# Channel maxima in one reduction per step: a gated mixture-of-experts kernel over NCHW images

## The reference

```python
def _L0_conv_ref(x, conv_w, conv_b):
    pooled = jnp.stack([jnp.max(x, axis=1), jnp.mean(x, axis=1)], axis=1)
    y = conv3x3(pooled, conv_w) + conv_b
    return x * jax.nn.sigmoid(y)

x = x + _L0_conv_ref(_ln_c(x), ...)
t = _to_tokens(x)
t = t + _L0_ffn_ref(_ln_t(t), ...)
```

## Time and profile before

| | us |
|---|---|
| median of 3 runs | 1582.37 (1581.99 to 1584.48) |
| the profiled execution, its own time | 1582.87 |
| its span, first to last instruction | 1581.1 |
| TensorE busy | 1432.2 |
| VectorE busy | 1326.6 |
| ScalarE busy | 1084.0 |
| GpSimd busy | 1072.8 |
| VectorE waiting for TensorE's spreads (line 665 for line 468) | 154.0 |
| TensorE waiting for VectorE's units (line 468 for line 665) | 91.0 |

### The profile page before, as it was taken

The page is one execution under the profiler, slowest core; times in us unless marked ns, Lnnn a source line. Parts: engine busy times, 40 slices in busy tenths (PEclk is TensorE's granted clock), DMA queues, the critical chain, the costliest instruction groups (busy, mean ns, idle before and its releaser), DMA issues.

```text
span 1581.1 us, 34381 instructions
## 1 busy us (share of the span) xinstructions
PE 1432.2 (91%) x12198; PEld 673.0 (43%) x12198; DVE 1326.6 (84%) x1647; ACT 1084.0 (69%) x4061; POOL 1072.8 (68%) x729
## 2 busy tenths in 40 slices
PE   8855998999898999899988998989998888899998
PEld 8753444444444444444434443444443232233333
DVE  6776898888898888889888888988888888887676
ACT  6667887778777887778877787778887334344432
POOL 5234776767676676677667676766766668787675
PEclk9955999999999999999999999999999899999999
DMA  6450565656556555556546565565554444455663
GB/s 215 124 144 20 176 187 153 187 176 193 158 153 199 176 177 180 166 179 188 179 149 187 176 199 153 154 198 179 180 176 133 135 144 142 140 165 169 180 178 114
DMA packets 85851, 260.04 MB, mean 164 GB/s; under 512 B 13744, under 2 KB 13744, under 8 KB 85680
## 3 DMA queue, kind: packets, MB, share of 16 engines
q1 hardware_dynamic: 85680, 257.85, 54.5%
HBM read 206.41 MB, written 51.38 MB: 163 GB/s over the span
## 4 chain that ended last, share of the span: by engine, by line
PE 66%; DVE 16%; issue 8%; ACT 2%; POOL 1%; DVEq 0%; ACTq 0%; POOLq 0%
PE moe L523 36%; PE gb L468 12%; DVE gx L665 8%; PE tm L447 7%; PE moe L517 4%; DVE quarter_key L696 3%; PE tm L507 3%; PE tm L461 2%; DVE key L692 2%; PE tm L547 1%; DVE stats L642 1%; DVE half_key L694 1%; ACT sq L928 1%; ACT logit_mean L994 0%; DVE u L762 0%
## 5 line engine op out<-in xcount | busy, mean ns | idle before, releaser
L523 PE MATMUL moe<-gx,wc 128*64 128x448 f32 x3584 | 843.8, 572 | 0.0
L665 DVE TENSOR_TENSOR gx<-gb,xd 128x896 f32<-128x896 f32 x672 | 711.1, 1086 | 157.6 <-PE gb L468 154.0
L1157 POOL TENSOR_TENSOR gx<-gs,xd 128x896 f32<-128x896 f32 x224 | 470.5, 2100 | 400.8 <-ACT gs L972 395.7
L972 ACT ACTIVATE gs<-gb 128x896 f32<-128x896 f32 x224 | 205.4, 917 | 249.4 <-PE gb L468 249.4
L468 PE MATMUL gb<-s,cg 54*128 54x448 bf16 x1792 | 260.3, 359 | 97.0 <-DVE gx L665 91.0
L928 ACT ACTIVATE sq<-xct 112x64 f32<-112x64 f32 x1400 | 337.9, 244 | 8.1 <-DVE early_s L652 2.6
L523 PEld LDWEIGHTS moe<-gx,wc 128*64 128x64 f32 x3584 | 224.8, 140 | 256.2 <-issue 203.6
L928 ACT ACTIVATION_READ_ACCUMULATOR sq<-xct 112x1 f32 x1400 | 263.1, 188 | 0.0
L1182 POOL TENSOR_TENSOR tt<-xc,a1s 128x896 f32<-128x896 f32 x112 | 236.3, 2110 | 12.5 <-issue 10.7
L468 PEld LDWEIGHTS gb<-s,cg 54*128 54x128 bf16 x1792 | 56.6, 94 | 439.9 <-DVE gx L665 330.4
L447 PEld LDWEIGHTS tm<-rhs,xa 64*112 64x112 f32 x2800 | 182.2, 192 | 29.6 <-issue 11.0
(11 more groups left out here) (96 smaller groups left out, 1334.2 us busy)
## 6 DMA issues: line engine op xcount, KB each, us to landing
xd<-in_x_dram SPq DMA_DIRECT2D x448, 224.0 KB, 4.0
xa<-in_x_dram SPq DMA_DIRECT2D x112, 448.0 KB, 4.4
xc<-in_x_dram SPq DMA_DIRECT2D x112, 448.0 KB, 4.8
out_dram<-ot SPq DMA_DIRECT2D x112, 448.0 KB, 3.3
gx<-in_const_g_dram SPq DMA_DIRECT2D x1, 384.0 KB, 4.6
cf<-in_const_f_dram SPq DMA_DIRECT2D x1, 332.5 KB, 2.8
gx<-in_L_ffn_expert_w_dram SPq DMA_DIRECT2D x1, 128.0 KB, 4.5
cf<-in_L_ffn_expert_b_dram SPq DMA_DIRECT2D x6, 2.0 KB
```

What stands on the lines that cost most here:

```text
L523: last = pe.matmul(moe[b * CH:(b + 1) * CH, c, 0:HALF], wc[:, k * CH:(k + 1) * CH], gx[:, u, b, :], start=False, stop=(k == KT - 1), skip_ ...
L665: dve.tensor_tensor(gx[:, i, :, :], gb[:, 2 * slot:2 * slot + 2, 0:HALF], xd[:, v % 2, :, c * HALF:(c + 1) * HALF], ALU.mult).then_inc(sca ...
L972: act.activation(gs[:, j, :, :], gb[:, 2:4, 0:HALF], ACT.Copy).then_inc(gate_out, 1)
L1157: pool.tensor_tensor(gx[:, ND + j, :, :], gs[:, j, :, :], xd[:, v % 2, :, j * HALF:(j + 1) * HALF], ALU.mult).then_inc(scaled_p, 1)
```

## The change

In the body of rounds 2 to 7, the maximum of group 0 is no longer taken in the middle of a step. At the end of the step, where the maximum of group 1 was taken, one `tensor_reduce` covers both groups: 1024 elements to 16 maxima. It waits for the copies of both groups and raises the semaphore `maxed` by 2 (NGRP). The early bodies keep the old form.

```diff
+            def channel_max_of_step(r, step):
+                if due(count := a_at(r, NGRP, step, NGRP)):
+                    dve.wait_ge(centred_out, count)
+                to, lo = stats_at(step)
+                if step == 0:
+                    if due(count := at(r, 0, JOINS, 0)):
+                        dve.wait_ge(joined, count)
+                dve.tensor_reduce(to[:, 0, lo:lo + 2 * ROWS], xct[:, step % 2, :, :], AX.X, ALU.max) \
+                   .then_inc(maxed, NGRP)
...
                         scale_unit(r, v, 2)
                         scale_unit(r, v, 3)
-                    if A:
-                        channel_max(r, step, 0)
 
                     if Bp:
                         gate(r, step, True)
...
                     if ahead:
                         scale_unit(r, v + 1, 0)
                     if A:
-                        channel_max(r, step, 1)
+                        channel_max_of_step(r, step)
```

## The result

The changed kernel takes 1627.17 us (1622.99 to 1631.29, four runs) against 1583.42 for the kernel before: a ratio of 1.0276, 95% interval 1.0238 to 1.0314, so 2.8% slower. The prediction was 1621 in a range of 1601 to 1645. The profiled execution took 1631.09 us with a span of 1629.3.

What follows compares the result with a forecast made beforehand. Ordinary half steps run at TensorE's pace; late VectorE router work stalls it. Stalls 13.8 + 24.0 + 4.8 + 1 = 43.6 us on 1582.87, less 5 for the clock and 0.5 for the median: 1621 us, range 1601 to 1645.

Steps and rivals of the forecast that it cites:

- Second halves: VectorE stretches after a step's first maximum: they lose 0.6 us of work, none is held by it, gain 0.
- Step 3: First half, after the previous step's second maximum: line 794 locked out by GpSimd's multiply; 2.3 us per round, 13.8 in all.
- Steps 8 and 12: First halves: line 717's subtraction comes 0.16 us too late and is locked out; 2.0 us each, 24.0 in all.
- Step 7: First key half: third and fourth key operations come behind GpSimd's multiply; 0.8 us later, 4.8 in all.
- Steps 9, 11, 13: Other key halves: the third key operation is locked by the multiply either way; 0, bounds 0 and 0.53 us.
- Steps 1 and 4: First halves: step 4's last router operation stays ahead of GpSimd's multiply; cost 0.1 us in each step.
- The clock: Granted clock around stalls: nothing charged for new stalls, three old ones keep their clock; -5 us.
- Rival (a): Shift counts, lock doesn't: each first half pays 0.53 us less its slack; +24, so 1606 us; chance 0.08.
- Rival (b): The clock falls after the new stalls as well; 1621 + 31 = 1652 us; chance 0.08.
- Rival (c): Faster: VectorE, ahead of the multiply in key halves, keeps GpSimd out across its short gaps; 1505 us; chance 0.02.
- Rival (d): The fixed cost saved by merging maxima reaches the end; -12.6, so 1570 us; chance 0.01.
- Rival (e): The halves are paced so that all of the change is hidden; 1582 us; chance 0.02.

Runs made afterwards that it cites:

- keep_middle: The changed kernel with the maximum of group 0 also taken again in the middle of the step, so computed twice; 1628.78 us, ratio to before 1.0274.
- short_7_11: The changed kernel with the old pair of maxima in steps 7 and 11 only; 1614.99 us, ratio to before 1.0199.
- gap_one_input: The changed kernel with the subtraction of line 727 replaced by a same-size reduction with one SBUF input; 1622.83 us, ratio to before 1.0248.
- longer_768: The kernel before with the maximum of group 1 over 768 elements, 0.27 us longer; 1611.39 us, ratio 1.0166.
- short_2_6_7_11: The changed kernel with the old pair of maxima in steps 2, 6, 7 and 11; 1585.25 us, ratio to before 1.0003.
- one_off_1: The kernel before with one reduction of constants ahead of unit 1 in step 3 of round 2, once in the run; 1589.39 us, ratio 1.0024.
- key_reduce_old_max: The kernel before with three of the four key operations replaced by one reduction with one SBUF input; 1488.46 us, ratio 0.9394.

## Why the prediction was right

- **Second halves: 0.** Held. keep_middle and the times of the second halves show no change in any of them that isn't the clock's.
- **Step 3: 2.3 us predicted, 2.26 measured**, by the way described: line 801 got in, GpSimd took the gap, line 804 waited for it. So in all six rounds.
- **Steps 8 and 12: 2.0 predicted, 1.94 measured.** Taken away by two edits that have nothing in common but the lock: an earlier issue (short_7_11) and one input less (gap_one_input).
- **Step 7: 0.8 predicted, 0.87 measured** where the clock doesn't blur it (keep_middle, 9.12 against 8.25).
- **Steps 9, 11, 13: 0 predicted, 0 measured.** Where the clock doesn't blur it, step 9 takes 8.45 us as before. The maximum that is 0.53 us longer meets a key operation that is 0.44 us shorter and a third one that waits for the multiply either way.
- **Steps 1 and 4: 0.1 each predicted**, 0.02 measured; too small to matter.
- The stalls by halves come to 6 x (2.26 + 2 x 1.94 + 0.87 + 0.02) = 42.2 us, where I had 43.6. The product of span and clock says 39. Over rounds 2 to 7 alone (first to last centring group, 1095.0 us before and 1146.3 after, at clocks of 0.954 and 0.947) it says 41, and behind them 1 less than before; the rest is within its scatter. In the view of waits TensorE waited for VectorE at line 468 for 91.0 us in 37 waits before and for 130.0 us in 54 after; I had forecast some 18 more. A round takes 191.2 us in three of the five full ones (194.4 and 189.7 in the others), where I had 191.
- **The clock: -5 predicted.** This is the term that was off, in its sign too. In the profiled execution the span grew by 48.2 us and the product by 39.1, so the clock (0.941 against 0.945) cost 9 us; in the run at 0.946 it cost 0.5. I was right in that old stalls lie at other moments and some keep their clock; the stall of step 13 did in all six rounds. But I charged nothing for stalls of about 2.2 us, and the old stall of step 0, 2.19 us as before, now loses the clock in rounds 3 to 7, where it never did, in two of them for a long stretch (8.64 us in the half behind it):

```profile
713.06 0.84 PE L468 MATMUL gb<-s,cg 54*128 54x448 bf16 x4 [2.19 <-DVE gx L675]
...
884.66 0.55 PE L468 MATMUL gb<-s,cg 54*128 54x448 bf16 x4 [2.58 <-DVE gx L675]
```

```profile
713.50:716.50 3.00, 3.00 (x24) 2.10 (x22) 2.43 (x4) 1.08 (x5) 1.12 (x2) 0.50 0.15 32
885.00:888.00 3.00, 3.00 (x32) 1.41 (x28) 2.73 (x5) 2.33 (x15) 0.19 (x1) 1.00 0.69 200
```

  The shorter stall (step 0, round 5) is followed by a clock of 0.50, the longer one (step 13) by 1.00. The new stall of step 3 lost the clock in two of six rounds, those of steps 8 and 12 (1.87 us in step 8 of round 5) in none of twelve. Two of the four runs had 0.946 and took 1623 us, two had 0.941 and 0.942 and took 1631; the prediction lies 2 us under the first pair. The stall term was a little too high and the clock term 5 to 14 us too low; that they partly made up for each other is luck.
- **Rival (a)**, length alone (1606), is refuted by the half times of gap_one_input and longer_768. **Rival (b)**, the clock lost at all new stalls (1652), didn't happen; a part did. **Rival (c)**, VectorE keeping GpSimd out across its gaps, is refuted by every key half of the changed kernel. **Rival (d)**, the saved fixed cost, is refuted by short_2_6_7_11 for the ten steps in which it had its chance. **Rival (e)**, that all is hidden (1582), is refuted by the time itself.

What stays open: what it is, beside its length, that makes a stall lose the clock. The runs show that there is something, not what.

## What to carry to other kernels

Before moving VectorE work by even half a microsecond, lay its operations with two SBUF inputs beside GpSimd's long ones: whether such an operation is issued 0.1 us before or behind a 2 us multiply decides over 2 us (longer_768: line 717 0.10 ahead and free, line 794 0.11 behind and locked out), and the length of what was moved says little about it. Where such an operation sits on the path, a form with one SBUF input, such as a reduction, can be longer and still win: here 6%. A high busy share can be waiting inside instructions; compare the same operation's shortest and longest duration first.

## What was not expected of the hardware

- The same stall of 2.19 to 2.20 us was followed by full clock in five of five rounds before, by half clock in five of five after, and by both in one kernel (one_off_1).
- Removing stalls gave back less than their length: 23.7 us of stalls gone in short_7_11, 12 us in the time; 20.7 and 4 in gap_one_input. In key_reduce_old_max it was the other way round, 57.7 and 95. A slow stretch costs 1.6 us and a long one 3.1, and their number changes with every edit.
- Of two operations that meet within 0.02 us (step 7 of longer_768), either can come first, and the round is 0.6 us shorter or longer by it.
- One delay of 0.72 us in the whole run went with a median 5 us longer (interval 0.06% to 0.42%, 1 to 7 us), the stalls elsewhere keeping their lengths.
